# Byte addresses worked out a block at a time, and one wait for two gather blocks, in a graph network's aggregation on Trainium2

## The reference

```
def _sage_layer(x, src, dst, inv_deg, W_self, W_neigh, b):
    agg = jax.ops.segment_sum(x[src], dst, num_segments=N_NODES)
    mean = agg * inv_deg[:, None]
    return x @ W_self + mean @ W_neigh + b
...
h = layernorm(x); h = relu(layer 0); h = relu(layer 1); h = layer 2; x = x + h
x = x + ffn(layernorm(x))    # gelu; only the rows that the router picks
```

## Time and profile before

| | us |
|---|---|
| median of 3 runs | 5516.28 |
| lowest and highest | 5500.15, 5523.34 |
| span of the profiled execution | 6674.4 |
| TensorE busy in it | 4538.9 (68%) |
| GpSimd busy | 3592.2 (54%) |
| VectorE busy | 2474.3 (37%) |
| ScalarE busy | 1087.1 (16%) |
| mean granted TensorE clock | 0.828 |

### The profile page before, as it was taken

One profiled execution on the slowest core, in us unless ns is written; L12 is line 12 of the kernel. 1 busy time (PEld: TensorE's weight loads), 2 busy tenths in 40 slices (PEclk: granted clock), 3 DMA queues, 4 the chain that ended last, 5 costly groups with the idle time before them and its releaser, 6 DMA issues.

```text
span 6674.4 us, 106521 instructions
## 1 busy us (share of the span) xinstructions
PE 4538.9 (68%) x21019; PEld 2870.7 (43%) x21020; DVE 2474.3 (37%) x6444; ACT 1087.1 (16%) x2645; POOL 3592.2 (54%) x3790
## 2 busy tenths in 40 slices
PE   0465566657897775567776656664788988778884
PEld 0122223225775442244552222321566765556664
DVE  7244444443333332112222223332333344444446
ACT  6000111111112120000000000110111232223331
POOL 0544454435554665666666666656666555655551
PEclk9667777778998887788897777776889998899997
DMA  9334444445665554566665555554555654444445
GB/s 305 111 112 122 127 136 138 118 116 179 206 216 151 152 151 142 164 188 192 202 196 147 145 151 153 154 143 141 175 183 187 195 153 128 139 130 137 132 133 185
DMA packets 569508, 1057.15 MB, mean 158 GB/s; under 512 B 145479, under 2 KB 377875, under 8 KB 559827
## 3 DMA queue, kind: packets, MB, share of 16 engines
q0 software_dynamic: 241920, 743.42, 39.1%
q10 hardware_dynamic: 213078, 267.53, 11.7%
q1 hardware_dynamic: 114429, 45.18, 2.6%
HBM read 907.18 MB, written 148.63 MB: 158 GB/s over the span
## 4 chain that ended last, share of the span: by engine, by line
PE 31%; issue 28%; another core or an unknown queue 11%; DVEq 10%; DVE 9%; POOL 4%; ACT 3%; DMA 2%; ACTq 1%; SPq 0%; POOLq 0%
PE agg L953 10%; POOL gath L726 4%; PE y L1043 3%; PE agg L955 3%; PE hid L1033 2%; PE y L785 2%; PE lo L955 2%; PE hid L889 2%; PE lo L889 2%; PE count_ps L889 2%; DVEq L1315 2%; DVEq L1335 2%; DVEq L1450 1%; DVE onehot L1315 1%
## 5 line engine op out<-in xcount | busy, mean ns | idle before, releaser
L726 POOL DMA_INDIRECT gath<-table,idx_ring x3780 | 3590.7, 950 | 2947.8 <-issue 1280.6
L953 PE MATMUL agg<-gath,onehot 128*128 x4896 | 2055.3, 448 | 1173.0 <-issue 865.0
L953 PEld LDWEIGHTS agg<-gath,onehot 128*128 x4896 | 531.3, 109 | 1961.8 <-issue 1663.0
L955 PE MATMUL agg<-gath,onehot 128*128 x3264 | 993.6, 304 | 134.9 <-issue 129.0
L1315 DVE TENSOR_TENSOR onehot<-count_ps,dst_f 128x512 f32 x607 | 419.7, 691 | 1500.9 <-remote 706.0
L1322 DVE TENSOR_SCALAR onehot<-iota_row,window_base,dst_f 128x128 f16 x1324 | 342.4, 331 | 981.6 <-remote 344.2
L955 PE MATMUL lo<-gath,onehot 128*128 x1632 | 536.9, 329 | 36.8 <-issue 34.9
L1043 PE MATMUL y<-w_sb,hidT 128*128 128x256 f32 x1568 | 406.5, 417 | 115.0 <-ACT hidT L1947 92.8
L955 PEld LDWEIGHTS agg<-gath,onehot 128*128 x3264 | 343.2, 105 | 326.8 <-issue 240.6
L1033 PE MATMUL hid<-featT,w_gnn 128*128 128x128 f32 x3136 | 400.3, 285 | 58.1 <-issue 57.5
L1033 PEld LDWEIGHTS hid<-featT,w_gnn 128*128 128x128 f32 x3136 | 383.4, 200 | 80.1 <-issue 71.6
(11 more groups left out here) (204 smaller groups left out, 4412.0 us busy)
## 6 DMA issues: line engine op xcount, KB each, us to landing
dense<-counts_dram ACTq DMA_DIRECT2D x75, 1024.0 KB
gath<-table,idx_ring POOLq DMA_INDIRECT x3780
table<-split ACTq DMA_DIRECT2D x194, 192.0 KB
dense<-rows_f ACTq DMA_DIRECT2D x72, 512.0 KB
counts_dram<-dense ACTq DMA_DIRECT2D x16, 1600.0 KB, 8.4
rows_f<-y ACTq DMA_DIRECT2D x194, 128.0 KB
table<-gath ACTq DMA_DIRECT2D x24, 768.0 KB, 8.4
xb<-x ACTq DMA_DIRECT2D x97, 128.0 KB
```

What stands on the lines that cost most here:

```text
L726: g.indirect_dma_start(gath[:, j, 0:PARTS * D], None, table[layer][:, :], bass.IndirectOffsetOnAxis(ap=idx_ring[:, h, i:i + 1], axis=0)).t ...
L953: mm(agg[p][:, 0:2 * D], oh, tile_rows[:, :, 0:2 * D], start=False, **flags)
L955: last = mm(low, oh, tile_rows[:, :, 2 * D:2 * D + lo_cols], start=False, **flags)
```

## The change

The rings (gath, onehot, low_hots, key_hots), the sorted destinations and the source ids are allocated as bytes, and bitcast where static views are wanted. Runtime operands are cut by byte offset and bitcast to their type (span_at). Helpers make the address registers at a chosen place ahead of the instruction that uses them: addressed for plain operands, counted for semaphore values, stationary for a matmul's stationary operand, whose last column is what is addressed. In a block, TensorE works out four one-hot addresses and the row addresses of the first two tiles, then waits for the one-hots, works out the other row addresses, then waits for the rows, then issues the eight matmuls. VectorE works out its addresses ahead of its wait for the slot. GpSimd waits once for each half of a turn, for both of its blocks, ahead of eight gathers.

```
+        def span_at(t, first, count, dt):
+            return t[:, bass.ds(first, count)].bitcast(dt)
+        def addressed(eng, *operands):
+            for operand in operands:
+                eng.lower_ap(operand)
+            return operands
+        def counted(eng, *values):
+            for value in values:
+                eng.lower_val(value)
+            return values
+        def stationary(eng, t, first, count):
+            eng.lower_ap(span_at(t, first + (count - 2), 2, BF16))
+            return span_at(t, first, count, BF16)
...
 def gather_turn(it, blocks):
     for h in range(2):
+        here = range(h * HALF_BLOCKS, min((h + 1) * HALF_BLOCKS, blocks))
         pool.wait_ge(idx_loaded[h], it * 16 + idx_base)
-        for q in range(h * HALF_BLOCKS, min((h + 1) * HALF_BLOCKS, blocks)):
-            pool.wait_ge(slots_free, it * RING_BLOCKS + q + free_base)
+        if here:
+            pool.wait_ge(slots_free, it * RING_BLOCKS + here[-1] + free_base)
             pool.sem_inc(pool_turn, 1)
+        for q in here:
             for j in range(q * GROUP, (q + 1) * GROUP):
...
 def count_tile(t, stop):
-    slot = pe.snap((t + g) % COUNT_RING)
-    pe.wait_ge(count_hots, t + g + 1)
-    return mm(count_ps[...], low_hots[:, bass.ds(slot, 1), :], key_hots[:, bass.ds(slot, 1), :], ...)
+    slot = (t + g) % COUNT_RING
+    hots_made, = counted(pe, t + g + 1)
+    lows = stationary(pe, low_hots, slot * HOT_BYTES, HOT_BYTES)
+    keys, = addressed(pe, span_at(key_hots, slot * KEY_BYTES, KEY_BYTES, BF16))
+    pe.wait_ge(count_hots, hots_made)
+    return mm(count_ps[...], lows, keys, ...)
...
 def block_products(b, last_block=False):
-    base = pe.snap((b % RING_BLOCKS) * GROUP)
-    pair = pe.snap(((b + w) % RING_BLOCKS) * GROUP)
-    pe.wait_ge(onehot_ready, b + w + pe_base[layer][0])
-    pe.wait_ge(rows_ready, b + pe_base[layer][1])
-    for j in range(GROUP):
-        oh = onehot[:, bass.ds(pair, GROUP), :][:, j:j + 1, :]
-        tile_rows = gath[:, bass.ds(base, GROUP), :][:, j:j + 1, :]
+    base = (b % RING_BLOCKS) * (GROUP * ROW_BYTES)
+    pair = ((b + w) % RING_BLOCKS) * (GROUP * HOT_BYTES)
+    hots_made, rows_there = counted(pe, b + w + pe_base[layer][0], b + pe_base[layer][1])
+    hots = [stationary(pe, onehot_bytes, pair + j * HOT_BYTES, HOT_BYTES) for j in range(GROUP)]
+    tiles = [addressed(pe, <512 columns>, <256 or 257 columns>) for j in range(GROUP // 2)]
+    pe.wait_ge(onehot_ready, hots_made)
+    tiles += [addressed(pe, <512 columns>, <256 or 257 columns>) for j in range(GROUP // 2, GROUP)]
+    pe.wait_ge(rows_ready, rows_there)
+    for j, (oh, (high_rows, low_rows)) in enumerate(zip(hots, tiles)):
...
 def block_onehots(b):
+    block_freed, = counted(dve, b + dve_base[layer])
     if ids is not None:
+        hots, tile_ids = addressed(dve, <one-hot ring>, <destinations>)
+        dve.wait_ge(slots_free, block_freed)
+        v.tensor_tensor(hots, ids..., tile_ids, ALU.is_equal).then_inc(onehot_ready, 1)
+        return
+    pairs = [addressed(dve, <one-hot tile>, <destinations>) for j in range(GROUP)]
+    dve.wait_ge(slots_free, block_freed)
...
 def tile_onehots(t):
+    slot_freed, = counted(dve, t + 2)
+    lows, low_id, keys, key_id, base = addressed(dve, ...)
+    dve.wait_ge(count_used, slot_freed)
```

More of the change, by code:

```diff
@@ L14 @@
 F16 = mybir.dt.float16
+U8 = mybir.dt.uint8
 P = 128
@@ L211, in gnn_ffn_program @@
         fin = [area[:, k * BATCH * D:(k + 1) * BATCH * D].rearrange("p (b d) -> p b d", d=D)
-               for area, bufs in ((dense[:], 6), (gath[:].rearrange("p r d -> p (r d)").bitcast(F32), 6), (dst_f[:], 1),
+               for area, bufs in ((dense[:], 6), (gath_bytes[:].bitcast(F32), 6), (dst_f[:], 1),
                                   (w1_sb.rearrange("p k n -> p (k n)"), 2), (w2_flat, 2),
@@ L944, in block_products @@
                 def block_products(b, last_block=False):
-                    base = pe.snap((b % RING_BLOCKS) * GROUP)
-                    pair = pe.snap(((b + w) % RING_BLOCKS) * GROUP)
-                    pe.wait_ge(onehot_ready, b + w + pe_base[layer][0])
-                    pe.wait_ge(rows_ready, b + pe_base[layer][1])
-                    for j in range(GROUP):
-                        oh = onehot[:, bass.ds(pair, GROUP), :][:, j:j + 1, :]
-                        tile_rows = gath[:, bass.ds(base, GROUP), :][:, j:j + 1, :]
+                    base = (b % RING_BLOCKS) * (GROUP * ROW_BYTES)
+                    pair = ((b + w) % RING_BLOCKS) * (GROUP * HOT_BYTES)
+                    hots_made, rows_there = counted(pe, b + w + pe_base[layer][0], b + pe_base[layer][1])
+                    hots = [stationary(pe, onehot_bytes, pair + j * HOT_BYTES, HOT_BYTES) for j in range(GROUP)]
+                    tiles = [addressed(pe, span_at(gath_bytes, base + j * ROW_BYTES, 4 * D, BF16),
+                                       span_at(gath_bytes, base + (j * ROW_BYTES + 4 * D), 2 * lo_cols, BF16))
+                             for j in range(GROUP // 2)]
+                    pe.wait_ge(onehot_ready, hots_made)
+                    tiles += [addressed(pe, span_at(gath_bytes, base + j * ROW_BYTES, 4 * D, BF16),
+                                        span_at(gath_bytes, base + (j * ROW_BYTES + 4 * D), 2 * lo_cols, BF16))
+                              for j in range(GROUP // 2, GROUP)]
+                    pe.wait_ge(rows_ready, rows_there)
+                    for j, (oh, (high_rows, low_rows)) in enumerate(zip(hots, tiles)):
                         flags = ends if last_block and j == GROUP - 1 else free
-                        mm(agg[p][:, 0:2 * D], oh, tile_rows[:, :, 0:2 * D], start=False, **flags)
+                        mm(agg[p][:, 0:2 * D], oh, high_rows, start=False, **flags)
                         low = agg[p][:, 0:D] if layer else agg_lo[:, 0:lo_cols]
-                        last = mm(low, oh, tile_rows[:, :, 2 * D:2 * D + lo_cols], start=False, **flags)
+                        last = mm(low, oh, low_rows, start=False, **flags)
                     return last
@@ L1308, in block_onehots @@
                 def block_onehots(b):
-                    pair, tiles = dve.snap(((b + w) % RING_BLOCKS) * GROUP), nc.s_assert_within(
-                        dve.snap((b + dve_skip0 * RING_BLOCKS) * GROUP), 0, (BLOCKS - 1) * GROUP,
+                    block = nc.s_assert_within(
+                        dve.snap(b + dve_skip0 * RING_BLOCKS), 0, BLOCKS - 1,
                         skip_runtime_bounds_check_because="blocks are counted from the sorted edges, below BLOCKS")
-                    dve.wait_ge(slots_free, b + dve_base[layer])
+                    pair, tiles = ((b + w) % RING_BLOCKS) * (GROUP * HOT_BYTES), block * (GROUP * ID_BYTES)
@@ L1314, in block_onehots @@
+                    block_freed, = counted(dve, b + dve_base[layer])
                     if ids is not None:
-                        v.tensor_tensor(onehot[:, bass.ds(pair, GROUP), :],
-                                        ids.unsqueeze(1).to_broadcast([P, GROUP, P]),
-                                        dst_f[:, bass.ds(tiles, GROUP)].unsqueeze(2).to_broadcast([P, GROUP, P]),
+                        hots, tile_ids = addressed(
+                            dve, span_at(onehot_bytes, pair, GROUP * HOT_BYTES, BF16).rearrange("p (g n) -> p g n", n=P),
+                            span_at(dst_bytes, tiles, GROUP * ID_BYTES, F32).unsqueeze(2).to_broadcast([P, GROUP, P]))
+                        dve.wait_ge(slots_free, block_freed)
+                        v.tensor_tensor(hots, ids.unsqueeze(1).to_broadcast([P, GROUP, P]), tile_ids,
@@ L1318, in block_onehots @@
                                         ALU.is_equal).then_inc(onehot_ready, 1)
                         return
+                    pairs = [addressed(dve, span_at(onehot_bytes, pair + j * HOT_BYTES, HOT_BYTES, BF16),
+                                       span_at(dst_bytes, tiles + j * ID_BYTES, ID_BYTES, F32))
+                             for j in range(GROUP)]
+                    dve.wait_ge(slots_free, block_freed)
                     dve.sem_inc(dve_turn, 1)
-                    for j in range(GROUP):
-                        last = v.tensor_scalar(onehot[:, bass.ds(pair, GROUP), :][:, j, :], iota_row[:],
-                                               window_base[:, col(w)], dst_f[:, bass.ds(tiles, GROUP)][:, j:j + 1],
+                    for hots, tile_ids in pairs:
+                        last = v.tensor_scalar(hots, iota_row[:], window_base[:, col(w)], tile_ids,
@@ L1436, in tile_onehots @@
                 def tile_onehots(t):
-                    slot = dve.snap((t + g) % COUNT_RING)
+                    slot = (t + g) % COUNT_RING
                     tile = nc.s_assert_within(
```

49 lines of the change are left out of this document (31 added, 18 removed).

## The result

The changed kernel is slower: 5647.73 us against 5513.11, four runs each, ratio 1.0245 (95% interval 1.0223 to 1.0267). The forecast was 5445; rival A (slower, the pair wait decides) had 5626.

What follows compares the result with a forecast made beforehand. The prediction took GpSimd's gather pace as the bound, with TensorE (and VectorE in layer 0) held up above it by address arithmetic. Terms -105 - 40 - 20 + 95 = -70 us gave 5446, say 5445 us, range 5390 to 5489.

Steps and rivals of the forecast that it cites:

- rival A: GpSimd's pair wait decides: 200 us more of TensorE's row waits against savings of 90, slower at 5626 us; chance 0.31.
- The floor: GpSimd's 3780 gathers at 1.25 us plus start, layer changes and end: no run below 5076 us.
- the fourth term: GpSimd's one wait for two blocks: 60 more TensorE row waits of 1.6 us, +95 us, bounds 0 to 300.
- the three savings: TensorE's block addresses, layer 0's count tiles and VectorE's one-hots: -105, -40 and -20 us, 165 together.
- a scale of 0.28: Plain-run stall over profiled stall, 440/1598; would shrink TensorE's 865.0 us of "issue" to 240.
- First term: TensorE's block addresses by bytes, ahead of the waits: 40% fewer register instructions, -105 us, bounds 0 to 260.
- The 350 us taken: Idle on "issue" ahead of TensorE's block matmuls in a plain run, assumed between 240 and 865 us.
- Second term: Layer 0's count tiles on TensorE and VectorE: 0.1 us less for each of 445 tiles, -40 us, bounds 0 to 92.
- Third, one-hots: VectorE's slot wait moves onto the comparison, so TensorE waits less for one-hots: about -20 us, bounds 0 to 60.
- the 6000 to 8000 named: Sign of being right: register instructions on TensorE's block matmul lines fall from 11016 to this range.
- GpSimd's waits for TensorE: Sign of being right: GpSimd's waits fall from 490 to some 300, with a longer mean.
- layer 0 gains from the addresses and layer 1 does not: Sign by layer: layer 0 should gain most, layer 1 least, having least stall and feeling the pair wait as much.

Runs made afterwards that it cites:

- experiment 1: Changed kernel with GpSimd's wait for each block put back before its four gathers, all address work kept: 5394.09 us, ratio 0.9809 to the kernel before.
- the pair wait alone: Kernel before with only GpSimd's wait changed to one for two blocks ahead of eight gathers: 5761.65 us, ratio 1.0470.
- experiment 8: experiment 1 with both waits of TensorE's block products ahead of all address work, which keeps its byte form: 5421.20 us, ratio 0.9865.
- the second recording of before: Kernel before, recorded again without any edit: span 5492.8 us, execution 5494.62 us.
- Experiment 9: Address work alone, with GpSimd waiting ahead of each two gathers, the first two on a new semaphore half_free: 5389.77 us, ratio 0.9795.
- pairs in one half: Changed kernel where only the first half of each turn waits for two blocks at once, the second block by block: 5548.45 us, ratio 1.0083.
- the wait for four: Changed kernel where GpSimd waits once a turn for all four blocks ahead of sixteen gathers: 7371.36 us, ratio 1.3406.

## Why the prediction was wrong

**The floor held.** Span less stall is 5492.8 - 433 = 5060 for before, 5389.4 - 330 = 5059 for experiment 1, 5652.2 - 595 = 5057 for the changed kernel, 5773.9 - 717 = 5057 for the pair wait alone. The other eight experiments lie between 5054 and 5064. The prediction had 5076 and a stall of 440. The gathers' pace is fixed, and every difference in this study shows as GpSimd standing still in the gather stretches.

**The step that failed is the fourth term, GpSimd's wait for two blocks: +95 forecast, 240 to 259 measured**, inside its bounds of 0 to 300. It said "the difference is one block's time", 1.3 us of packed tiles, and took "60 more" waits of 1.6 us. There are 79 more waits for rows (285 to 364, both with the new addresses), and they hold 230 us more, 2.9 each. Two blocks do not come free a block's matmul time apart but 5.1 us at the median, across window work, dense work or a wait for rows. GpSimd then stood 2.9 us longer at 174 pairs, where the upper bound had 1.5 us at 122 and 5 us more at one in ten. Of the 205 us between the forecast change (-70) and the measured one (+135), this term holds 145 and the three savings, 165 forecast and 105 measured, hold 60.

**What led it there.** The prediction's argument against rival A was "rows are late only 38 times now". That count is of the stretched recording; the second one has 270. TensorE was already waiting for rows in many places, so a gather that starts later could cost time there. The prediction saw that the recording was 21% above the median and weighed a scale of 0.28 for the sizes of its waits, but kept who waits for whom. It is just this that the stretch had changed. That the recording "makes the sequencers' work larger" is no property of recording this program: the second one does not.

**First term, TensorE's addresses: -105 forecast, 32 +-11 measured.** The 350 us taken for "issue" were 56.9. The count fell further than assumed: a block had 10.2 register instructions and has 3.2 (12522 and 3954 in all, by the two traces), 68% fewer where 40% was forecast. So the count was no measure of the gain. The prediction weighed the Trainium skill here (Perfetto Trace Analysis, section Sequencer Loop: a waiting engine instruction sits in its queue, a control instruction is executed by the sequencer) and took from it that the term would be nearer 260. The size is not borne out, 32 against 260. That the place of a wait matters agrees with experiment 8, 31 +-12 us.

**Second term, count tiles: -40 forecast, 63 +-11 measured.** The mechanism (tile by tile in turn, nearly all on the path) was right, the 0.1 us a tile too small at 0.14. **Third, one-hots: -20 forecast, 28 +-11 measured.** Its own numbers, 93 x 0.2 + 11, give 30 and not 20. The three were to be 165 and are 105 together. Rival A had 90 for them and 200 for the wait, 5626; it was right in kind, and low by 22 us because both parts were larger, 105 and 240.

**The other signs.** Register instructions fell further than the 6000 to 8000 named. GpSimd's waits for TensorE did not fall: 224 in the second recording of before, 225 after, with a mean of 2.6 us in place of 2.0. The span fell while the median rose, but only because before's first recording was stretched. That layer 0 gains from the addresses and layer 1 does not is right (stall 334 to 230, 19 to 19, 80 to 81), and so is that all layers feel the pair wait alike (+83, +95, +87 from experiment 1 to the changed kernel).

**The version to keep** is experiment 1, 0.9809 (0.9795 to 0.9822) of before. Experiment 9 adds a semaphore and nothing that can be measured.

## What to carry to other kernels

When a recording is much longer than the plain runs, record again before reading its waits: a slowed sequencer changes not only how long they are but which of them exist. In a ring of few slots like this one, a wait for several slots can cost the time between their releases, which is set by whatever work stands between their last uses, not by the time of a slot's own work. Count the register arithmetic that stands where two engines hand single items to and fro, or behind a wait: here 1336 instructions of the first kind were worth 63 us and 8568 in the block products 32, about as much as their place behind the waits alone.

## What the runs showed of the hardware

**The same program's register instructions ran slower in one recording.** In before's first recording 1089 of TensorE's and 837 of VectorE's sequencer instructions took 0.64 to 0.76 us, in the second 5 and 11, with the same 22619 and 18188 instructions. What caused it stays open.

**When rows come late, matmuls also run at a lower clock.** The mean granted clock is 0.901 in experiment 1, 0.886 with pairs in one half, 0.877 in the changed kernel and 0.790 with the wait for four. The same 21019 matmuls are busy for 4056 us in experiment 1 and for 4160 in the changed kernel. The timeline above shows it in small: ahead of the 7.15 us idle a matmul of line 998 takes 0.38 us, right behind it 0.61. The stretches before, right after, and one window's work later (columns as in rows 4):

```profile
2434.00:2443.70 9.70, 8.41 (x44) 6.10 (x41) 3.35 (x7) 0.40 (x1) 6.56 (x7) 1.00 0.52 143
2451.00:2453.40 2.40, 2.40 (x8) 1.11 (x8) 0.00 (x0) 0.00 (x0) 1.79 (x3) 0.50 1.00 345
2457.10:2458.60 1.50, 1.50 (x12) 0.98 (x10) 0.00 (x0) 0.92 (x3) 0.00 (x0) 1.00 0.00 0
```

The granted clock is 1.00 (2.4 GHz) while TensorE works, 0.50 (1.2 GHz) in the block after the idle time, and 1.00 again 4 us later. This is frequent but not the rule: in the changed kernel 164 of the 364 waits for rows are followed by a line 998 matmul of over 0.5 us, in experiment 1 121 of 285. Between these two recordings the span grows by 263 us, TensorE's busy time by 104 and its idle time by 159. How much of the 240 us is the clock and how much the rows alone, no run here parts.
